# A vision-transformer block on one core: the remainder matmuls over the last 64 features, as pairs of 64-row tiles

## The chip, the cores and the metric

The kernel runs on one core of one Trainium2 chip. The metric is the device time of one execution in microseconds. The core has five engines with queues of their own: TensorE multiplies matrices (a weight load, then a matmul that streams columns against the loaded weights), VectorE and ScalarE work element by element, GpSimd does small work and indirect DMAs, SyncE issues DMAs. They are ordered among each other by semaphores that the kernel sets and waits for by hand.

## What is computed

Sixteen images of 3 x 112 x 112 are cut into 49 patches of 16 x 16 each; every patch becomes a token of 192 features. Then follow a self-attention with 12 heads of 64 and a feed-forward layer with 8 experts, of which each token goes to two. Cut to what matters:

```python
h = tok(x)                                   # [16, 49, 192], patches @ conv_w + position
y = layernorm(h)
q, k, v = y @ W_Q + b_Q, y @ W_K + b_K, y @ W_V + b_V
h = h + softmax(causal(q @ k.T / 8)) @ v @ W_O + b_O
x = layernorm(h)
top_p, top_i = top_k(softmax(x @ gate_w.T), 2)
for e in range(8):                           # up to 245 rows of one expert
    z = rms_norm(2 * rows[e]) * norm_w[e]
    g, u = split(z @ w13[e].T)               # 2 x 512 columns
    rows[e] = rows[e] + (silu(g) * u) @ w2[e].T
out = h + weighted sum of each token's two rows
```

## The kernel before

Tokens are worked on in 8 pairs of images, 98 tokens each (`PT`); the pairs 0 to 3 and 4 to 7 are the two halves. The 192 features are split in 128 (`DA`) and 64 (`DR`).

**Split products.** The products with W_Q, W_K, W_V and w13 take rounded 32-bit operands (f32r) in two pieces: a rounded value, and the rest that rounding left. The product of 128 features is made of three matmuls: value x value, value x rest, rest x value. For the last 64 features the pieces are stacked over the 128 partitions. `yR` (and `zeR` for the experts) holds the rounded values in the partitions 0 to 63 and the rests in 64 to 127; the weight tile `[.., 0, 1, ..]` holds the rounded weights twice, one copy above the other, and `[.., 1, 1, ..]` the rests of the weights, twice as well. One matmul with the first gives value x value and value x rest of the weights' values at once; a second one, with the second tile, adds rest x value, and rest x rest, which would not be needed.

So each output tile takes five matmuls. In `values(p)` (lines 340 to 344) they are for two banks of 384 columns each. In `queries_keys(half)` (L366 to L370) they are for 12 groups per half, 6 of queries and 6 of keys, of 400 columns each; the groups go round four banks of PSUM (0, 1, 4, 5), and a group waits for the evacuation of the group four before it. In `gate_up(e)` (L525 to L531) they are for 4 tiles `jt` of 128 hidden features, each with a gate and an up part (`u` 0 and 1) of 246 columns (`EC`) in one bank.

**Who makes the pieces.** ScalarE copies and rounds: `y_hi(p)` (L593, L594) after the transposes of y, and `x_hi(e)` (L717, L718) after those of the expert's rows. VectorE subtracts: `y_lo(p)` (L875, L876) and `x_lo(e)` (L1041, L1042). GpSimd clears `yA` and `yR` at the start (L760, L761).

**Who takes the results.** ScalarE evacuates the queries (L603) and values (L634) and applies silu to the gates (L724), VectorE evacuates the keys (L884) and multiplies gate and up (L1047). Each waits for a semaphore that the last matmul of the group raises: `qk_done`, `v_done`, `gu_done`.

**The order on TensorE.** Convolution of the pairs 0 to 3, transposes of y, some matmuls on a filler tile (L457), `queries_keys(0)`, and then a loop of steps s. A step has the transposes of the softmax for pair s (L393), the scores of pair s + 2 (L381 for the mask, over the whole array, and L386, 64 x 64 tiles, two heads side by side), the values of pair s + 1, the output projection of pair s - 1 (L416), the weighting with the values for pair s (L406, 64 x 64 tiles, two heads and two images at once), and small work for the choice of experts. Behind `values` stand L406 for five pairs, and for the pairs 0, 2 and 3 the matmuls L449, L416 and L327. `queries_keys(1)` runs in step 2, between. After all steps the rows come back from the scatter, and the experts run: `gate_up(0)`, then for each e `gate_up(e + 1)`, `transpose_x(e + 2)` (L511, L512) and `down(e)` (L544, 16 matmuls). The matmuls over plain 32-bit data (L386, L393, L406, L416, L544) show as two instructions for each call, except the transposes.

**The order on ScalarE in the expert stage.** For each e: `silu(e + 1, jt)` for four jt, with `split_hi(e + 2, jt)` (L669) behind the first two, then `x_hi(e + 2)` and `weigh(e)` (L736). VectorE has `gated`, `split_lo` and `x_lo` likewise. `gate_up(e)` waits for `x_hi` before its first matmul and for `x_lo` before its third (L529).

Of the kernel before, what the change touches and what calls it, by code (L numbers as in the profile page):

```python
# [22 lines left out]
TOK = PER_SIDE * PER_SIDE  # L23
D = 192
DA, DR = 128, 64
# [8 lines left out]
PT = 2 * TOK  # L34
# [20 lines left out]
def vit_block(nc, patches, conv_w, w_qkv, w_o, w13, w2, by_column, by_row, before, masking, blank, zeros, numbers, out):  # L55
# [6 lines left out]
    with ExitStack() as ctx:  # L62
# [30 lines left out]
        y = sb("y", [PT, 2, D])  # L93
        yA = sb("yA", [128, 2, PH, 128], f32r)
        yR = sb("yR", [128, PH, 128], f32r)
        qT = sb("qT", [128, HP, PH, 2, SLOT])
        kT = sb("kT", [128, HP, PH, 2, TOK])
        v = sb("v", [128, PH, QKV])
# [47 lines left out]
        toke = sb("toke", [EROWS, EXPERTS, 2], u32)  # L146
        zeA = sb("zeA", [128, 2, 2, EC], f32r)
        zeR = sb("zeR", [128, 2, EC], f32r)
        tokens_row = sb("tokens_row", [EROWS, N])
        member = sb("member", [EROWS, len(ONCHIP), N], f32r)  # L150
        yo = sb("yo", [EROWS, len(ONCHIP), 2, D], f32r)
# [150 lines left out]
        def _(pe):  # L302
# [27 lines left out]
            def values(p):  # L330

                pe.wait_ge(wlo_ready, 3)
                pe.wait_ge(ylo_ready, p + 1)
                if p >= 1:
                    pe.wait_ge(pt_ready, p)
                q = p % PH
                for j in range(2):
                    c = slice(384 * j, 384 * (j + 1))
                    o = ps[:, 2 + j, 0:384]
                    mm(o, yA[:, 0, q, :], wqkv[:, 2, 0, 0, c], start=True, stop=False)  # L340
                    mm(o, yA[:, 0, q, :], wqkv[:, 2, 1, 0, c], start=False, stop=False)
                    mm(o, yA[:, 1, q, :], wqkv[:, 2, 0, 0, c], start=False, stop=False)
                    mm(o, yR[:, q, :], wqkv[:, 2, 0, 1, c], start=False, stop=False)
                    last = mm(o, yR[:, q, :], wqkv[:, 2, 1, 1, c], start=False, stop=True)
                last.then_inc(v_done, 1)

            def queries_keys(half):

                pe.wait_ge(ylo_ready, PH * (half + 1))
                for n in range(2 * HP):  # L350
                    w, hp = n // HP, n % HP
                    if half and n == 2:
                        pe.wait_ge(z_ready, PH - 1)
                    if not half and hp == 0:
                        pe.wait_ge(wlo_ready, w + 1)
                    if n >= 4:
                        if n - 4 < HP:
                            pe.wait_ge(q_ready, HP * half + n - 3)
                        else:
                            pe.wait_ge(k_ready, HP * half + n - 3 - HP)  # L360
                    c = slice(128 * hp, 128 * (hp + 1))
                    o = ps[:, (0, 1, 4, 5)[n % 4], 0:2 * PH * EVEN].rearrange("p (s t) -> p s t", t=EVEN)

                    def tokens(t):
                        return t.rearrange("p a (i s) -> p (a i) s", i=2)[:, :, 0:EVEN]
                    mm(o, wqkv[:, w, 0, 0, c], tokens(yA[:, 0]), start=True, stop=False)  # L366
                    mm(o, wqkv[:, w, 0, 0, c], tokens(yA[:, 1]), start=False, stop=False)
                    mm(o, wqkv[:, w, 1, 0, c], tokens(yA[:, 0]), start=False, stop=False)  # L368
                    mm(o, wqkv[:, w, 0, 1, c], tokens(yR[:]), start=False, stop=False)  # L369
                    mm(o, wqkv[:, w, 1, 1, c], tokens(yR[:]), start=False, stop=True).then_inc(qk_done, 1)  # L370

            def scores(p):
                if p >= 1:
# [141 lines left out]
            def gate_up(e):  # L515
# [3 lines left out]
                for jt in range(JT):  # L519
                    if e >= 1:  # L520
                        pe.wait_ge(hT_ready, JT * (e - 1) + jt + 1)
                    for u in range(2):
                        o = ps[:, 2 + jt, u * EC:(u + 1) * EC]
                        w = slice(u * HID + 128 * jt, u * HID + 128 * (jt + 1))
                        mm(o, wsp[:, j, 0, 0, w], zeA[:, j, 0, :], start=True, stop=False)  # L525
                        mm(o, wsp[:, j, 1, 0, w], zeA[:, j, 0, :], start=False, stop=False)  # L526
                        if jt == 0 and u == 0:
                            pe.wait_ge(zelo_ready, e + 1)
                        mm(o, wsp[:, j, 0, 0, w], zeA[:, j, 1, :], start=False, stop=False)  # L529
                        mm(o, wsp[:, j, 0, 1, w], zeR[:, j, :], start=False, stop=False)  # L530
                        last = mm(o, wsp[:, j, 1, 1, w], zeR[:, j, :], start=False, stop=True)  # L531
                    last.then_inc(gu_done, 1)

            def down(e):
                j = e % 2
# [47 lines left out]
        def _(act):  # L583
# [6 lines left out]
            def y_hi(p):  # L590
                act.wait_ge(yt_done, p + 1)
                q, bank = p % PH, yt_bank(p)
                A(yA[:, 0, q, :].rearrange("q (i s) -> q i s", i=2)[:, :, 0:TOK], ps[:, bank, 0:PT].rearrange("q (i t) -> q i t", i=2), ACT.Copy)  # L593
                A(yR[0:DR, q, :].rearrange("q (i s) -> q i s", i=2)[:, :, 0:TOK], ps[0:DR, bank, 128:128 + PT].rearrange("q (i t) -> q i t", i=2),  # L594
                  ACT.Copy).then_inc(yhi_ready, 1)

            def queries_keys(half, some):
                for n in some:
# [115 lines left out]
            def x_hi(e):  # L714
                j = e % 2
                act.wait_ge(et_done, e + 1)
                A(zeA[:, j, 0, :], ps[:, j, 0:EC], ACT.Copy, scale=raw13[j][:, 2 * W13:2 * W13 + 1])  # L717
                A(zeR[0:DR, j, :], ps[0:DR, j, EC:2 * EC], ACT.Copy, scale=raw13[j][0:DR, 2 * W13 + 1:2 * W13 + 2]).then_inc(zehi_ready, 1)  # L718

            def silu(e, jt):  # L720
                act.wait_ge(gu_done, JT * e + jt + 1)
# [34 lines left out]
        def _(pool):  # L756
            P = nc.gpsimd
            P.memset(filler[:], 0.0).then_inc(filler_ready, 1)  # L758
            P.memset(mhalf[:], -0.5)
            P.memset(yA[:].bitcast(f32), 0.0)  # L760
            P.memset(yR[:].bitcast(f32), 0.0).then_inc(y_zeroed, 1)  # L761
            P.memset(qT[:], 0.0)
            P.memset(prob[:], 0.0)
# [394 lines left out]
```

## Time and profile before

| | |
|---|---|
| median of 3 runs | 217.92 us (217.6 to 218.06) |
| the profiled execution, its own time | 216.08 us |
| its span, from the first instruction to the last | 214.3 us |
| TensorE matmuls, busy | 193.9 us (91%), 1926 instructions |
| TensorE weight loads, busy | 175.6 us (82%) |
| VectorE busy | 125.3 us (58%) |
| ScalarE busy | 90.6 us (42%) |
| GpSimd busy | 66.8 us (31%) |
| TensorE's share of the chain that ended last | 75% |

In the rows below PE is the matmul part of TensorE, PEld its weight loads, DVE is VectorE, ACT ScalarE, POOL GpSimd; a q behind one is its queue. L with a number is the line of the kernel. Matmuls are pipelined and their ends are modelled: two that follow each other overlap in the rows, and busy time is not the same as time at full rate. The page of this profile gives the shares of the whole span; for the three edited places the views by stretch, and the starts of single instructions in them, say more.

### The profile page before, as it was taken

The page shows a single profiled execution, that of the slowest core. Times are in us where ns is not written, and L with a number is a line of the kernel's source. Part 1 is how long each engine was busy: PE and PEld are TensorE (multiplying, and loading weights), DVE is VectorE, ACT ScalarE, POOL GpSimd, SP SyncE. Part 2 cuts the span into 40 slices and gives each one's busy share as a digit, 9 for nine tenths or more (in the row PEclk, how much of TensorE's full clock was granted, in tenths as well). Part 3 has the DMA queues.
Part 4 walks back from the last instruction along what each step waited for, and adds up shares of the span by engine and source line. Part 5 has one row for each costly group of instructions (what it writes and reads, how often), then busy time and mean ns, then how long its engine had stood idle before and what let it go on. Part 6 is the DMA issues. An engine that isn't in the chain of part 4 may idle for free.

```text
span 214.3 us, 4932 instructions
## 1 busy us (share of the span) xinstructions
PE 193.9 (91%) x1926; PEld 175.6 (82%) x1926; DVE 125.3 (58%) x381; ACT 90.6 (42%) x186; POOL 66.8 (31%) x114
## 2 busy tenths in 40 slices
PE   6878999999989998999999859299999999999970
PEld 1865998998988996989999734289999999999960
DVE  0369365766465055997775872454584486495174
ACT  2064601215335511365487553156476567653110
POOL 9531000120135000266366877000225315514000
PEclk9999999999999999999999999979999999999996
DMA  6999990000014000001101001257187678513633
GB/s 191 401 401 432 309 360 24 2 3 0 3 25 163 35 3 0 14 20 33 32 0 32 26 23 27 85 188 279 18 313 244 204 254 266 161 32 110 161 67 114
DMA packets 11204, 27.07 MB, mean 126 GB/s; under 512 B 2661, under 2 KB 6498, under 8 KB 9998
## 3 DMA queue, kind: packets, MB, share of 16 engines
q1 hardware_dynamic: 8366, 24.10, 32.6%
q0 software_dynamic: 2304, 2.21, 3.7%
q10 hardware_dynamic: 512, 0.46, 0.8%
q8 instruction: 15, 0.25, 0.5%
q14 instruction: 7, 0.06, 0.1%
HBM read 23.95 MB, written 5.77 MB: 139 GB/s over the span
## 4 chain that ended last, share of the span: by engine, by line
PE 75%; DVE 7%; POOL 7%; DMA 4%; issue 4%; ACT 1%; DVEq 0%; SPq 0%; POOLq 0%; ACTq 0%
PE ps L544 10%; PE ps L386 6%; PE ps L416 6%; PE ps L314 5%; POOL slots L811 4%; PE ps L529 4%; PE ps L530 3%; PE ps L531 3%; PE ps L526 3%; PE ps L525 3%; PE ps L406 3%; PE ps L366 2%; DMA xp<-patches 2%; PE ps L368 2%; PE ps L369 2%
## 5 line engine op out<-in xcount | busy, mean ns | idle before, releaser
L836 POOL DMA_INDIRECT parts<-qT,toke x12 | 17.2, 1430 | 44.2 <-ACT qT L736 42.4
L811 POOL DMA_INDIRECT slots<-row,slot x16 | 18.0, 1122 | 29.2 <-issue 22.9
L974 DVE TENSOR_TENSOR wqkv<-raw,wqkv 128x1024 fp32r<-128x1024 f32 x16 | 19.5, 1222 | 7.6 <-DMA slots<-row,slot 4.4
L1047 DVE TENSOR_TENSOR v<-v,ps 128x246 f32<-128x246 f32 x32 | 12.5, 407 | 19.2 <-ACT v L724 19.2
L544 PE MATMUL ps<-xp,v 128*123 128x192 f32 x128 | 22.0, 326 | 0.0
L544 PEld LDWEIGHTS ps<-xp,v 128*123 128x123 f32 x128 | 20.6, 186 | 0.0
L525 PE MATMUL ps<-zeA,wqkv 128*128 128x246 f32 x64 | 19.0, 297 | 0.0
L630 ACT ACTIVATE prob<-sm 128x588 f32<-128x588 f32 x8 | 5.6, 706 | 31.0 <-DVE sm L895 31.0
L314 PE MATMUL ps<-convw,xp 128*98 128x192 f32 x96 | 16.9, 330 | 1.8 <-DMA xp<-patches 1.0
L724 ACT ACTIVATE v<-ps 128x246 f32<-128x246 f32 x32 | 12.0, 375 | 14.9 <-PE ps L531 13.4
L457 PE MATMUL ps<-filler 128*128 128x512 bf16 x62 | 17.1, 427 | 1.3 <-POOL filler L758 1.3
L529 PE MATMUL ps<-zeA,wqkv 128*128 128x246 f32 x64 | 18.0, 282 | 0.0
L531 PE MATMUL ps<-zeR,wqkv 128*128 128x246 f32 x64 | 17.9, 280 | 0.0
L530 PE MATMUL ps<-zeR,wqkv 128*128 128x246 f32 x64 | 17.9, 280 | 0.0
L526 PE MATMUL ps<-zeA,wqkv 128*128 128x246 f32 x64 | 17.8, 279 | 0.0
L314 PEld LDWEIGHTS ps<-convw,xp 128*98 128x98 f32 x96 | 15.1, 165 | 3.0 <-DMA xp<-patches 1.9
L416 PE MATMUL ps<-wo,zs 128*98 128x192 f32 x96 | 17.2, 329 | 0.0
L669 ACT ACTIVATE wqkv<-raw 128x1024 fp32r<-128x1024 f32 x16 | 16.9, 1053 | 0.0
L416 PEld LDWEIGHTS ps<-wo,zs 128*98 128x98 f32 x96 | 15.1, 165 | 0.7 <-issue 0.4
L884 DVE TENSOR_SCALAR kT<-ps,columns 128x392 f32<-128x392 f32 x12 | 7.5, 626 | 13.8 <-PE ps L370 13.8
L774 POOL TENSOR_SCALAR ve<-mv 98x1 f32<-98x1 f32 x8 | 2.2, 269 | 41.8 <-DVE mv L861 41.8
L386 PEld LDWEIGHTS ps<-kT,qT 64*64 64x64 f32 x384 | 12.4, 134 | 2.7 <-issue 1.2
(143 smaller groups left out, 483.8 us busy)
## 6 DMA issues: line engine op xcount, KB each, us to landing
raw<-w SPq DMA_DIRECT2D x8, 1025.0 KB, 6.3
xp<-w SPq DMA_DIRECT2D x8, 384.0 KB
xp<-patches SPq DMA_DIRECT2D x8, 294.0 KB, 5.8
raw<-w_qkv SPq DMA_DIRECT2D x3, 768.0 KB, 9.0
slots<-blank SPq DMA_DIRECT2D x8, 196.0 KB, 4.5
xp<-slots SPq DMA_DIRECT2D x8, 196.0 KB
parts<-zeros SPq DMA_DIRECT2D x1, 1176.0 KB, 8.7
part<-parts SPq DMA_DIRECT2D x4, 294.0 KB
```

Of the source, the lines that this page charges most:

```text
L314: last = mm(ps[0:PT, conv_bank(p), 0:D], xp[:, p % PH, c, :], convw[:, c, :], start=(c == 0), stop=(c == KC - 1))
L386: last = mm(ps[r, hp // 3, c:c + TOK], qT[r, hp, p % PH, i, :], kT[r, hp, p % PH, i, :], start=False, stop=(hp % 3 == 2 and i == 1))
L416: last = mm(ps[0:PT, 6, 0:D], zs[:, p % 2, c, :], wo[:, c, :], start=(c == 0), stop=(c == HP - 1))
L525: mm(o, wsp[:, j, 0, 0, w], zeA[:, j, 0, :], start=True, stop=False)
L526: mm(o, wsp[:, j, 1, 0, w], zeA[:, j, 0, :], start=False, stop=False)
L529: mm(o, wsp[:, j, 0, 0, w], zeA[:, j, 1, :], start=False, stop=False)
L530: mm(o, wsp[:, j, 0, 1, w], zeR[:, j, :], start=False, stop=False)
L531: last = mm(o, wsp[:, j, 1, 1, w], zeR[:, j, :], start=False, stop=True)
L544: last = mm(ps[0:EROWS, 6 + r, 0:D], hT[:, j, jt, r * EROWS:(r + 1) * EROWS], w2s[:, j, jt, :], start=(jt == 0), stop=(jt == JT - 1))
L811: P.indirect_dma_start(slots, bass.IndirectOffsetOnAxis(slot[:, p % PH, k:k + 1], 0), row[:, p % 2, k, :], None, bounds_check=EXPERTS * ST ...
L836: P.indirect_dma_start(parts, bass.IndirectOffsetOnAxis(toke[:, e, r:r + 1], 0), ye[0:EROWS, e % 2, r, :], None, bounds_check=TOPK * N + E ...
L974: last = V.tensor_tensor(wsp[:, j, 1, half, :], raw13[j][:, half * W13:(half + 1) * W13], wsp[:, j, 0, half, :].bitcast(f32), ALU.subtract)
```

## The change

Of the five matmuls of a group the last, with the rests of the weights, gives up its rest x rest half: only the 64 rows with the rounded values are left. Two groups' last matmuls are made a pair, one on the partitions 0 to 63 and one on 64 to 127, each with an output bank of its own. For the second the rounded values have to lie in the partitions 64 to 127, which is what the new tiles `yH` and `zeH` are for: ScalarE writes the same rounded values a second time. Pairs are: in `values` the two banks; in `queries_keys` groups n and n + 1; in `gate_up` the tiles jt and jt + 1, once for the gate and once for the up part. The semaphores of both groups of a pair are raised behind the pair, so the first group of a pair is released later than before. In `gate_up` only the first group in a bank starts with the flag that clears it, since both groups of a bank are open at the same time. GpSimd clears `yH` too.

```diff
@@ -93,6 +93,7 @@
         yR = sb("yR", [128, PH, 128], f32r)
+        yH = sb("yH", [128, PH, 128], f32r)
@@ -146,6 +147,7 @@
         zeR = sb("zeR", [128, 2, EC], f32r)
+        zeH = sb("zeH", [128, 2, EC], f32r)
@@ -341,8 +343,8 @@
                     mm(o, yR[:, q, :], wqkv[:, 2, 0, 1, c], start=False, stop=False)
-                    last = mm(o, yR[:, q, :], wqkv[:, 2, 1, 1, c], start=False, stop=True)
-                last.then_inc(v_done, 1)
+                mm(ps[:, 2, 0:384], yR[0:DR, q, :], wqkv[0:DR, 2, 1, 1, 0:384], start=False, stop=True)
+                mm(ps[:, 3, 0:384], yH[DR:128, q, :], wqkv[DR:128, 2, 1, 1, 384:768], start=False, stop=True).then_inc(v_done, 1)
@@ -367,7 +369,10 @@
                     mm(o, wqkv[:, w, 0, 1, c], tokens(yR[:]), start=False, stop=False)
-                    mm(o, wqkv[:, w, 1, 1, c], tokens(yR[:]), start=False, stop=True).then_inc(qk_done, 1)
+                    if n % 2:
+                        mm(pair, wqkv[0:DR, w, 1, 1, 128 * (hp - 1):128 * hp], tokens(yR[0:DR]), start=False, stop=True).then_inc(qk_done, 1)
+                        mm(o, wqkv[DR:128, w, 1, 1, c], tokens(yH[DR:128]), start=False, stop=True).then_inc(qk_done, 1)
+                    pair = o
@@ -522,14 +527,20 @@
-                        mm(o, wsp[:, j, 0, 0, w], zeA[:, j, 0, :], start=True, stop=False)
+                        mm(o, wsp[:, j, 0, 0, w], zeA[:, j, 0, :], start=(u == 0), stop=False)
...
-                        last = mm(o, wsp[:, j, 1, 1, w], zeR[:, j, :], start=False, stop=True)
-                    last.then_inc(gu_done, 1)
+                    if jt % 2:
+                        for u in range(2):
+                            w = [slice(u * HID + 128 * t, u * HID + 128 * (t + 1)) for t in (jt - 1, jt)]
+                            o = [ps[:, 2 + t, u * EC:(u + 1) * EC] for t in (jt - 1, jt)]
+                            first_of = mm(o[0], wsp[0:DR, j, 1, 1, w[0]], zeR[0:DR, j, :], start=False, stop=(u == 1))
+                            second = mm(o[1], wsp[DR:128, j, 1, 1, w[1]], zeH[DR:128, j, :], start=False, stop=(u == 1))
+                        first_of.then_inc(gu_done, 1)
+                        second.then_inc(gu_done, 1)
@@ -591,8 +602,9 @@
-                A(yR[0:DR, q, :].rearrange("q (i s) -> q i s", i=2)[:, :, 0:TOK], ps[0:DR, bank, 128:128 + PT].rearrange("q (i t) -> q i t", i=2),
-                  ACT.Copy).then_inc(yhi_ready, 1)
+                for rows_of in (yR[0:DR], yH[DR:128]):
+                    last = A(rows_of[:, q, :].rearrange("q (i s) -> q i s", i=2)[:, :, 0:TOK], ps[0:DR, bank, 128:128 + PT].rearrange("q (i t) -> q i t", i=2), ACT.Copy)
+                last.then_inc(yhi_ready, 1)
@@ -715,7 +727,9 @@
-                A(zeR[0:DR, j, :], ps[0:DR, j, EC:2 * EC], ACT.Copy, scale=raw13[j][0:DR, 2 * W13 + 1:2 * W13 + 2]).then_inc(zehi_ready, 1)
+                for rows_of in (zeR[0:DR], zeH[DR:128]):
+                    last = A(rows_of[:, j, :], ps[0:DR, j, EC:2 * EC], ACT.Copy, scale=raw13[j][0:DR, 2 * W13 + 1:2 * W13 + 2])
+                last.then_inc(zehi_ready, 1)
@@ -758,6 +772,7 @@
             P.memset(yA[:].bitcast(f32), 0.0)
+            P.memset(yH[:].bitcast(f32), 0.0)
             P.memset(yR[:].bitcast(f32), 0.0).then_inc(y_zeroed, 1)
```

## Rows read from the trace of the kernel before

**Rows 1.** The page, part 4: shares of the chain that ended last.

```profile
PE 75%; DVE 7%; POOL 7%; DMA 4%; issue 4%; ACT 1%; DVEq 0%; SPq 0%; POOLq 0%; ACTq 0%
```

**Rows 2.** Busy time by stretch, and TensorE's granted clock (PEclk, 1.00 is full).

```profile
core 0: us, PE busy (x) PEld busy (x) DVE busy (x) ACT busy (x) POOL busy (x), PEclk, DMA share, GB/s
20.20:31.90 11.70, 11.70 (x62) 11.27 (x60) 6.46 (x10) 4.68 (x8) 0.00 (x0) 1.00 0.97 347
...
141.00:204.00 63.00, 63.00 (x503) 63.00 (x502) 35.90 (x77) 33.81 (x72) 17.16 (x12) 0.99 0.59 191
```

**Rows 3.** The chain in order of time, attention: start, length in us, what.

```profile
99.60 0.85 PE ps L406 x48
...
102.70 0.83 PE ps L386 x24
```

**Rows 4.** Timeline, matmuls of `gate_up`: start, duration, engine, line, operation, shapes.

```profile
155.79 0.28 PE L531 MATMUL ps<-zeR,wqkv 128*128 128x246 f32 x1
...
156.37 0.28 PE L531 MATMUL ps<-zeR,wqkv 128*128 128x246 f32 x1
```

**Rows 5.** Timeline, matmuls of `queries_keys(0)`, one group.

```profile
22.02 0.35 PE L366 MATMUL ps<-yA,wqkv 128*128 128x400 f32 x1
...
22.98 0.36 PE L366 MATMUL ps<-yA,wqkv 128*128 128x400 f32 x1
```

**Rows 6.** Timeline, the end of `values` and the first 64 x 64 tiles behind.

```profile
90.62 0.34 PE L343 MATMUL ps<-wqkv,yR 128*128 128x384 f32 x1
90.80 0.34 PE L344 MATMUL ps<-wqkv,yR 128*128 128x384 f32 x1
91.06 0.45 PE L406 MATMUL ps<-probT,v 64*64 64x49 f32 x16
```

**Rows 7.** Groups by line and shape: count, busy us, mean ns of one, idle before.

```profile
L531 PE MATMUL ps<-zeR,wqkv 128*128 128x246 f32 x64 | 17.9, 280 | 0.0
...
L386 PE MATMUL ps<-kT,qT 64*64 64x49 f32 x384 | 14.4, 221 | 0.0
...
L344 PE MATMUL ps<-wqkv,yR 128*128 128x384 f32 x16 | 5.4, 337 | 0.0
```

**Rows 8.** Timeline, from the last 64 x 64 tiles to full matmuls.

```profile
37.80 0.22 PE L386 MATMUL ps<-kT,qT 64*64 64x49 f32 x2
37.95 0.44 PE L340 MATMUL ps<-wqkv,yA 128*128 128x384 f32 x1
38.23 0.33 PE L341 MATMUL ps<-wqkv,yA 128*128 128x384 f32 x1
```

**Rows 9.** A transpose behind 64 x 64 tiles (timeline), and the mean (groups).

```profile
82.96 0.33 PE L393 MATMUL ps<-columns,prob 128*128 128x128 f32 x1
...
L393 PE MATMUL ps<-columns,prob 128*128 128x128 f32 x48 | 6.7, 276 | 0.0
```

**Rows 10.** Timeline, `y_hi(7)` and the start of `queries_keys(1)`.

```profile
68.40 0.25 ACT L593 ACTIVATE yA<-ps 128x98 fp32r<-128x98 f32 x1
...
68.54 0.24 ACT L594 ACTIVATE yR<-ps 64x98 fp32r<-64x98 f32 x1
...
69.39 0.46 PE L366 MATMUL ps<-yA,wqkv 128*128 128x400 f32 x1 [0.36 <-DVE yR L876]
```

**Rows 11.** Timeline, `y_lo(3)` and the start of `queries_keys(0)`.

```profile
19.66 0.26 DVE L876 TENSOR_TENSOR yR<-ps,yR 64x98 fp32r<-64x98 f32 x1
...
20.01 0.43 PE L366 MATMUL ps<-yA,wqkv 128*128 128x400 f32 x1
```

**Rows 12.** Timeline, `x_hi` and `x_lo` of one expert, and their reader.

```profile
159.19 0.45 ACT L718 ACTIVATE zeR<-ps,raw 64x246 fp32r<-64x246 f32 x1
...
160.18 0.47 DVE L1042 SCALAR_TENSOR_TENSOR zeR<-ps,raw,zeR 64x246 fp32r<-64x246 f32 x1
...
161.46 0.28 PE L529 MATMUL ps<-zeA,wqkv 128*128 128x246 f32 x1
```

**Rows 13.** Timeline, GpSimd at the start.

```profile
2.12 0.53 POOL L761 MEMSET yR<- 128x512 f32 x1
...
9.36 0.19 POOL L774 TENSOR_SCALAR ve<-mv 98x1 f32<-98x1 f32 x1 [1.81 <-DVE mv L861]
```

## The prediction

> **What bounds the kernel now.** I read the chain of work that ended last first. TensorE carries three quarters of it, in small shares by line [rows 1]. So the second view is the busy time by stretch: in the first stretch of query and key matmuls (the second is alike) and in the whole expert stage TensorE is busy all of the time, at a granted clock of 1.00 and 0.99, while VectorE and ScalarE are busy for little over half of it at most [rows 2]. Between these the attention steps run nearly back to back on TensorE too: the chain there is TensorE's lines one after the other [rows 3]. The reader is to see that nearly every nanosecond that TensorE's queue gains or loses in the three edited places ends in the time, and that what other engines get on top is mostly under cover.
>
> **How the durations are read.** A matmul's duration is longer than what it occupies, since the next one starts while it drains. So the cadence counts, the distance of two starts: 0.58 us from L531 to the next L531 five matmuls on, 0.115 each [rows 4]; 0.96 for five of the 400-column matmuls of queries and keys, 0.192 each [rows 5]; 0.175 for the 384-column ones of `values` [rows 6]. The durations are 0.280 and 0.337 [rows 7] and 0.355 [rows 5], and they count wherever something has to wait for the end.
>
> **What the change removes.** 64 matmuls L531 become 64 of 64 rows, which run as 32 rounds of two; 24 of L370 become 12 rounds; 16 of L344 become 8 rounds. That two row halves do run side by side is seen in the trace: 48 matmuls L406, on four quarters of the array with outputs in two banks, take 0.85 us, 24 of L386 on two quarters take 0.83 [rows 3]. A pair of L386 so takes about twice the time per instruction of L406: what is set is the time of a round, not of an instruction. I take a round to have the cadence of the full matmul it replaces, since its 128 weight columns and its streamed columns are the same. The Trainium skill, page "TensorE: Matmul & The Clock Gate", section "LDWEIGHTS (loading the stationary operand)", says the same of the weights: the load goes by columns and not by rows; no row here separates the two.
>
> **What it adds: a change of the array's division, in and out.** The trace has some fifty places where a full matmul is followed by one on a quarter of the array or the other way round, and each has a gap. The last L344 at 90.80, first L406 at 91.06 [rows 6]: 0.27 where the cadence is 0.175. Last L386 at 37.80, first full matmul L340 at 37.95 [rows 8]: 0.15, where rounds of the same kind are some 0.06 apart (0.83 for twelve, of which 0.15 is the way out [rows 3]). Both gaps are the duration of the matmul before less 0.07 (0.337 - 0.07, 0.221 - 0.07 [rows 7]): the next one starts only when the array is nearly empty. And then its weights were not loaded ahead: L340 after the gap lasts 0.44, not 0.337, and the one behind it starts 0.28 later, not 0.175 [rows 8]. So each such change costs (duration - 0.07 - cadence) plus 0.10 of open weight load. Behind it L393, a transpose, shows only 0.33 for 0.276, so 0.05 [rows 9].
> The skill's page "TensorEngine Tiling (Array Packing)", section "Key Properties", puts it as a rule, and against this change: changing the tiling mode drains the TensorE. The trace agrees, with the 0.27 and 0.15 above. No row shows a tile of 64 rows by 128 columns, only 64 by 64; I take the same price, as the nearest row. Both ends for it: nothing, if halves by rows alone need no change (the first rival), and 0.10 for the weights in full.
>
> **Experts, L525 to L531.** Two blocks per expert, 16 in all. From the last full matmul to the first tile 0.21 + 0.10, second round 0.115, its second tile 0.01 later, then to the next full one 0.21 + 0.10: 0.745 us. Before, the same stretch held five cadences (one of its own and four L531): 0.575. So +0.17, x16 = 2.7. Behind six of the blocks stand the transposes of `transpose_x`, which show 0.05 and not 0.10: -0.3. Sum +2.4.
>
> **Queries and keys, L366 to L370.** 12 blocks of one round: 0.285 + 0.10, + 0.01, + 0.285 + 0.10 = 0.78, against three cadences, 0.58. +0.20, x12 = 2.4; the last block of each half is followed by the bf16 mask L381, whose weights are short (no open load taken): -0.2. Sum +2.2.
>
> **Values, L340 to L344.** 8 blocks. Three (p = 0, 2, 3) are followed by full matmuls: 0.37 + 0.01 + 0.37 = 0.75 against 0.525, +0.22 each, less about 0.1 in all for shorter weights behind: +0.6. Five are followed by L406, which pays its gap already now: 0.37 + 0.01 + 0.27 = 0.65 against 0.62, +0.03 each, +0.1 (if going from one kind of tile to another needs no gap, -0.1 each instead). Sum +0.7.
>
> **The second copy.** On ScalarE each `y_hi` and each `x_hi` gets one more activation. (a) `y_hi(7)`: its L593 and L594 (68.40, 68.54) stand in the chain to L366, which waited 0.36 us for `y_lo` [rows 10]; the three activations would start 0.14 apart as these two do, so +0.15. (b) `y_hi(3)`: its `y_lo` ended at 19.91, and L366 started at 20.01 behind the fillers [rows 11], so at most 0.1 of cover stands against 0.15 asked, and the weight load comes later too: +0.1. (c) `x_hi`, in every expert: L718 at 159.19; `x_lo` ends at 160.65 (L1042), and L529, which waits for it, starts at 161.46: 0.8 us of cover [rows 12]. (d) GpSimd's memset of `yH` is like that of `yR`, 0.53 us; GpSimd then waited 1.81 us for its first moments [rows 13], so nothing; without that cover 0.5. Together +0.3 for (a) and (b).
> The moved semaphores add no wait, but eat cover: `silu` of tiles 0 and 2 now wait for the next tile too. Queued behind the silu of tile 2 on ScalarE are that of tile 3 and `x_hi`; both silus start when the last tile is done. That puts `x_hi` back by about 0.2 and its third activation adds 0.36, while TensorE comes 0.1 later; of the 0.8 some 0.3 is left. If it were gone, six experts would pay what is missing. The next user of a bank in `gate_up` of the next expert comes over 2.6 us later (`down`, 16 of L544, lies between). In `queries_keys` banks are four deep: group n+4 starts a whole pair (1.9 us) after the release of n and n+1, whose two evacuations take some 1.2.
>
> **Sum.** 2.4 + 2.2 + 0.7 + 0.3 = +5.6 us. The profiled execution took 216.1 (span 214.3, 1.8 around it) and becomes 221.7; the median of the runs is 217.92 and becomes 223.5.
>
> **Rivals.**
> 1. No drain between whole rows and row halves (the tile is as wide as the array, and only the 64 by 64 ones pay). Then each round replaces two matmuls for good: 32 x 0.115 + 12 x 0.192 + 8 x 0.175 = 3.7 + 2.3 + 1.4 = 7.4 less, 0.3 for the copy: 217.9 - 7.1 = 210.8. For it: only 64 by 64 tiles are in the trace. Against: every change there, in and out, with bf16, f32 and rounded f32 neighbours, has the gap. It decides as soon as a block costs less than the two or four cadences that it frees, which is at about 0.17 us (experts) and 0.20 us less than the price taken. The time by the skill's table "Theoretical Speedup" of the tiling page (up to 2x for 64 rows) would be this one. Chance 0.12.
> 2. The drain, but weights loaded under it. Of 36 ways in and some 22 ways out with wide weights, 0.10 each, up to 5.8 us go: between 217.7 and 221, say 220. Against: the load of L340 is open after its gap [rows 8]. Chance 0.10.
> 3. The two halves don't run side by side, since each now takes all columns of the array. Then every round pays its cadence twice: +7.4 on the forecast, 230.9. For: L406 and L386 share the columns by halves. Against: in L406 upper and lower rows feed the same columns, in two banks, and still four run at once [rows 3]. Chance 0.05.
> Forecast with its mechanism: 0.73; its own range 221.5 to 225.5 (a fifth of each gap either way, and the cover of (c)).
>
> **Chances and range.** Less than 0.2% of 218 us, 0.4 us, a measurement of this kernel can't tell from no change. Faster: the first rival and a little of the second's lower end, 0.13. Same: 0.03, from that lower end. Slower: 0.84. The range reaches down over most of the second rival and up a little past the forecast's own: 219.0 to 226.5; left out are the first and third rival and the second's lowest end.
>
> **What would show it.** In the changed profile: starts of the row tiles, pairs 0.01 apart (else rival 3); 0.31 from L530 to where the first tile really streams and 0.21 from the last tile to the next full matmul (else rival 1); the matmul behind it at 0.38 instead of 0.28 (else rival 2). The way from one `down` to the next becomes 0.3 longer. TensorE's granted clock stays at 1.00 in these stretches; if it fell to half, all of this would be wrong. A wait of L529 for `zelo_ready` would show (c) gone.

## The result and the profile after

| | before | after |
|---|---|---|
| median (lowest to highest) | 217.99 us (217.6 to 218.17, 4 runs) | 223.35 us (222.45 to 224.28, 4 runs) |
| profiled execution, its own time | 216.08 us | 224.08 us |
| its span | 214.3 us | 222.1 us |

The ratio is 1.0249, 95% interval 1.0193 to 1.0304: slower, by 5.4 us in the medians, and clear of no change; that it is 2% or more is likely and not sure. The two profiled executions lie 8.0 us apart, and of that 1.7 are a matter of the start, as the table of stages shows.

The page of after, parts 1 and 4, first lines. Against [rows 1] the chain is made of the same engines.

```profile
PE 201.6 (91%) x1923; PEld 170.8 (77%) x1926; DVE 124.9 (56%) x381; ACT 94.8 (43%) x202; POOL 67.1 (30%) x115
...
PE 76%; DVE 7%; POOL 6%; DMA 4%; issue 4%; ACT 1%; DVEq 0%; SPq 0%; POOLq 0%; ACTq 0%
```

Busy time of after by stretch: first queries and keys, second, expert stage, as in [rows 2].

```profile
21.90:34.50 12.60, 12.55 (x61) 9.77 (x60) 5.88 (x8) 4.72 (x8) 0.00 (x0) 1.00 0.89 316
73.10:85.60 12.50, 12.50 (x60) 9.74 (x60) 2.32 (x4) 3.70 (x9) 0.35 (x1) 1.00 0.04 15
146.00:206.80 60.80, 60.80 (x458) 56.24 (x456) 36.36 (x77) 35.72 (x77) 17.03 (x12) 1.00 0.55 182
```

The matmul side is as full as before, and that is what misleads here: the weight loads, 11.27 of 11.70 us in [rows 2], are now 9.77 of 12.60. TensorE is not waiting for anybody there; it is between two ways of using its array. The granted clock is 1.00 in these three stretches.

One block of `gate_up` in after, by the timeline (start, duration, engine, line). It answers to [rows 4].

```profile
160.97 0.28 PE L534 MATMUL ps<-zeA,wqkv 128*128 128x246 f32 x1
161.09 0.27 PE L535 MATMUL ps<-zeR,wqkv 128*128 128x246 f32 x1
161.29 0.38 PE L540 MATMUL ps<-zeR,wqkv 64*128 64x246 f32 x1
161.29 0.38 PE L541 MATMUL ps<-zeH,wqkv 64*128 64x246 f32 x1
161.51 0.27 PE L540 MATMUL ps<-zeR,wqkv 64*128 64x246 f32 x1
161.51 0.28 PE L541 MATMUL ps<-zeH,wqkv 64*128 64x246 f32 x1
161.71 0.38 PE L530 MATMUL ps<-zeA,wqkv 128*128 128x246 f32 x1
161.94 0.27 PE L531 MATMUL ps<-zeA,wqkv 128*128 128x246 f32 x1
```

Read the starts: 0.20 from the last full matmul to the first tile, where the cadence is 0.115; the two tiles of a round start together; the second round 0.22 later, since the first tile's weights were loaded in the open (0.38 for 0.27); 0.20 to the next full one, again with its load in the open. From L535 to the second full matmul behind, 0.85 us; before, six cadences, 0.69.

One block of `queries_keys` and one of `values`, the same view; they answer to [rows 5] and [rows 6].

```profile
23.39 0.35 PE L371 MATMUL ps<-yR,wqkv 128*128 128x400 f32 x1
23.67 0.45 PE L373 MATMUL ps<-yR,wqkv 64*128 64x400 f32 x1
23.67 0.45 PE L374 MATMUL ps<-yH,wqkv 64*128 64x400 f32 x1
24.06 0.46 PE L368 MATMUL ps<-yA,wqkv 128*128 128x400 f32 x1
24.36 0.35 PE L369 MATMUL ps<-yA,wqkv 128*128 128x400 f32 x1
```

```profile
51.48 0.34 PE L345 MATMUL ps<-wqkv,yR 128*128 128x384 f32 x1
51.74 0.44 PE L346 MATMUL ps<-wqkv,yR 64*128 64x384 f32 x1
51.75 0.44 PE L347 MATMUL ps<-wqkv,yH 64*128 64x384 f32 x1
52.12 0.39 PE L411 MATMUL ps<-probT,v 64*64 64x49 f32 x12
```

The last row shows that from tiles of 64 x 128 to tiles of 64 x 64 the array empties as well: 0.37, of which 0.10 is the 64 x 128 tile's own open load.

The stages, from the starts of their first instructions in the two timelines, in us (the 5.9 ahead of the first convolution and the 6.7 between the first and the second row are alike in both and left out):

| stage | before | after | difference | forecast |
|---|---|---|---|---|
| first convolution to the first transposes of y | 5.93 | 7.62 | +1.69 | 0 |
| `y_hi(3)`: its transposes to the first queries | 1.47 | 1.73 | +0.25 | +0.1 |
| `queries_keys(0)` | 11.67 | 12.70 | +1.03 | +1.1 |
| steps up to `queries_keys(1)`, with four `values` and `y_hi(7)` | 37.71 | 38.44 | +0.73 | +0.8 |
| `queries_keys(1)` | 11.44 | 12.68 | +1.24 | +1.1 |
| steps up to the experts, with four `values` | 57.12 | 57.23 | +0.11 | +0.1 |
| first transposes of rows to the first `gate_up` | 2.56 | 2.98 | +0.42 | 0 |
| first `gate_up` to `combine` | 58.46 | 60.92 | +2.46 | +2.4 |
| the rest, from `combine` on | 15.31 | 15.23 | -0.08 | 0 |

Three rows hold differences that the edit did not make. The first is taken up below. In `queries_keys(1)` of before five matmuls take 0.945 us where they take 0.967 in `queries_keys(0)`, and four of the other profiles with the same five matmuls there have 11.70 us for the stage and not 11.44. Against those the changed kernel's 12.68 is +1.0, as in the first half. And at the head of the expert stage TensorE ran at its lower rate in both, but not over the same matmuls: in after for all eight transposes of rows (0.20 us apart), in before for the last of them (0.10 apart until then) and into the first `gate_up`.

### The profile page after: what moved, and what is told of

Same layout as the page of the kernel before. It is cut to its first block, busy times and chain, and to the rows that moved or that the text cites. A ratio compares the mean times of both kernels' runs of the same rounds, so it can differ in the third digit from the quotient of the medians.

```text
span 222.1 us, 4946 instructions
## 1 busy us (share of the span) xinstructions
PE 201.6 (91%) x1923; PEld 170.8 (77%) x1926; DVE 124.9 (56%) x381; ACT 94.8 (43%) x202; POOL 67.1 (30%) x115
## 4 chain that ended last, share of the span: by engine, by line
PE 76%; DVE 7%; POOL 6%; DMA 4%; issue 4%; ACT 1%; DVEq 0%; SPq 0%; POOLq 0%; ACTq 0%
PE ps L555 9%; PE ps L391 6%; PE ps L421 6%; PE ps L316 6%; PE ps L530 4%; PE ps L534 4%; POOL slots L826 4%; PE ps L531 3%; PE ps L535 3%; PE ps L368 3%; PE ps L540 3%; PE ps L411 2%; DMA xp<-patches 2%; PE ps L370 2%; PE ps L369 2%
## 5 line engine op out<-in xcount | busy, mean ns | idle before, releaser
L1062 DVE TENSOR_TENSOR v<-v,ps 128x246 f32<-128x246 f32 x32 | 12.2, 406 | 21.6 <-issue 11.1
L989 DVE TENSOR_TENSOR wqkv<-raw,wqkv 128x1024 fp32r<-128x1024 f32 x16 | 19.5, 1222 | 7.7 <-DMA slots<-row,slot 4.4
L316 PE MATMUL ps<-convw,xp 128*98 128x192 f32 x96 | 18.6, 352 | 1.8 <-DMA xp<-patches 1.0
L530 PE MATMUL ps<-zeA,wqkv 128*128 128x246 f32 x64 | 19.7, 307 | 0.0
L316 PEld LDWEIGHTS ps<-convw,xp 128*98 128x98 f32 x96 | 16.5, 179 | 3.3 <-DMA xp<-patches 1.9
L738 ACT ACTIVATE v<-ps 128x246 f32<-128x246 f32 x32 | 10.9, 373 | 18.1 <-PE ps L541 14.1
L534 PE MATMUL ps<-zeA,wqkv 128*128 128x246 f32 x64 | 18.5, 289 | 0.0
L531 PE MATMUL ps<-zeA,wqkv 128*128 128x246 f32 x64 | 17.7, 277 | 0.0
L535 PE MATMUL ps<-zeR,wqkv 128*128 128x246 f32 x64 | 17.7, 277 | 0.0
L462 PE MATMUL ps<-filler 128*128 128x512 bf16 x59 | 16.3, 425 | 1.5 <-POOL filler L772 1.3
L899 DVE TENSOR_SCALAR kT<-ps,columns 128x392 f32<-128x392 f32 x12 | 7.0, 621 | 17.5 <-PE ps L374 17.5
L391 PE MATMUL ps<-kT,qT 64*64 64x49 f32 x384 | 14.4, 221 | 0.0
```

The lines of the kernel that those rows point to most:

```text
L316: last = mm(ps[0:PT, conv_bank(p), 0:D], xp[:, p % PH, c, :], convw[:, c, :], start=(c == 0), stop=(c == KC - 1))
L391: last = mm(ps[r, hp // 3, c:c + TOK], qT[r, hp, p % PH, i, :], kT[r, hp, p % PH, i, :], start=False, stop=(hp % 3 == 2 and i == 1))
L530: mm(o, wsp[:, j, 0, 0, w], zeA[:, j, 0, :], start=(u == 0), stop=False)
L989: last = V.tensor_tensor(wsp[:, j, 1, half, :], raw13[j][:, half * W13:(half + 1) * W13], wsp[:, j, 0, half, :].bitcast(f32), ALU.subtract)
```

## The experiments

Theory: the loss is in the passages, TensorE emptying its array and loading weights in the open on the way into the tiles and out of them. Rivals: it is ScalarE's second copy with the later semaphores; or the row tiles don't gain side by side what was counted. Stages are compared inside the profiles; the medians have a spread of their own, which the last runs explain in part.

**The copies alone.** To the kernel before only this is added (and `yH` cleared):

```diff
+                for rows_of in (yR[0:DR], yH[DR:128]):
+                    last = A(rows_of[:, q, :]...)
...
+                for rows_of in (zeR[0:DR], zeH[DR:128]):
+                    last = A(rows_of[:, j, :]...)
```

> Only the second copy: yH and zeH are written by ScalarE (and yH cleared by GpSimd), and nobody reads them; all matmuls are those of the kernel before. Theory of the passages (the loss is TensorE changing the array's division, emptying it and loading weights in the open each time): +0.4 us against before in the profiled span, 0.26 at the start of the first queries and keys, 0.12 to 0.15 at the second, nothing in the expert stage. Rival (ScalarE's extra activations and the later semaphores carry the loss): most of the +6, of it 2 or more in the expert stage.

Measured: ratio 1.0032 (0.9993 to 1.0070). From the transposes of y (pair 3) to the first queries +0.26 us, as expected; the stretch up to the second queries and keys +0.26, twice what was expected; first `gate_up` to `combine` 58.46, as before. So in attention the copies carry 0.5 us.

That the expert stage shows nothing is chance. Here TensorE ran at full rate from the first transpose of rows on (granted clock 1.00 in the 4 us behind it), and in before it didn't (0.60 in 138 to 141 us). The fair comparison is a kernel of further below, with the five matmuls of before and full rate in this stretch. The third matmul of the first `gate_up`, which waits for `x_lo(0)`, comes 2.53 us after the first transpose there and 3.01 here, where a third activation stands ahead of `x_lo(0)`. The rows of the waits, first that kernel, then this one:

```profile
PE ps L529 <- DVE zeR L1042: 0.3, 1, 0.3
...
PE ps L531 <- DVE zeR L1048: 0.5, 1, 0.5
```

From the first transposes of rows to `combine` it is 60.03 us there and 60.48 here: +0.45, once. The copies carry up to 1 us, and still not the six.

**The expert stage alone.** Attention is as before; `zeH` and the pairs in `gate_up` are those of the change.

> The change in the expert stage alone (zeH, 16 blocks of two rounds); attention as before. Passages: from first gate_up to the end of the last one +0.16 us for each of 16 blocks, about 0.3 less in all for the transposes behind six of them: +2.3 to 2.6 us in the span. Rival (copies and semaphores): the same size here but as waits of TensorE inside the stage; there should be none.

Measured: ratio 1.0143 (1.0062 to 1.0224). First `gate_up` to `combine` +2.47, as in the whole change (+2.46), so the edits in attention and in the experts don't act on each other. The waits have no row for TensorE in this stage, as expected.

**Twice as many blocks, the same tiles.**

```diff
                     for u in range(2):
                         ... four full matmuls
+                        if jt % 2:
+                            ... the two tiles of this u
```

> Expert stage alone, the pair for the gates and the pair for the ups each as a block of its own behind its matmuls: 32 blocks of one round instead of 16 of two, the same matmuls. Passages: a block costs 0.31 to get in, 0.31 to get out and frees two cadences of 0.115, so +0.27 each against before, x32 = +8.7, less 0.3 for the transposes: +8.4 us against before, about +6 against the experts-only kernel with 16 blocks. Rival (copies and semaphores): as the 16-block kernel, +2.4. Rival (row tiles are slow by themselves): as the 16-block kernel, since the tiles are the same.

```profile
150.91 0.28 PE L531 MATMUL ps<-zeR,wqkv 128*128 128x246 f32 x1
151.12 0.38 PE L535 MATMUL ps<-zeR,wqkv 64*128 64x246 f32 x1
151.12 0.38 PE L536 MATMUL ps<-zeH,wqkv 64*128 64x246 f32 x1
151.43 0.38 PE L526 MATMUL ps<-zeA,wqkv 128*128 128x246 f32 x1
```

Measured: ratio 1.0365 (1.0285 to 1.0446); the stage +8.18 us. The timeline above has a block of one round: 0.21 in, 0.31 to the next full matmul. Same tiles, same copies, same work, only 32 blocks for 16: the loss goes with the number of passages, 5.7 us for 16 more, 0.36 each. (The kernel with 16 blocks has a second loss in its +2.47, told below; by single `gate_up` of the experts 2 to 6 it is 4.73 to 4.76 us before, 4.94 to 4.96 with two blocks and without that loss, 5.70 to 5.72 with four: 0.38 a block.)

**Both tiles on the same rows.**

```diff
-    second = mm(o[1], wsp[DR:128, j, 1, 1, w[1]], zeH[DR:128, j, :], ...)
+    second = mm(o[1], wsp[0:DR, j, 1, 1, w[1]], zeR[0:DR, j, :], ...)
```

> Expert stage alone, 16 blocks, but both tiles of a round take the upper 64 rows (zeR and the weights of the partitions 0 to 63; the result is the same, zeH is written and not read). So the two of a round can't run side by side. Passages, with rounds that overlap in the real change: two tiles a cadence of 0.115 apart instead of 0.003, two times a block: +0.23 a block, x16 = +3.6 us on top of the experts-only kernel, +6 against before. If the two halves do not run side by side anyway: no difference to the experts-only kernel.

```profile
147.56 0.28 PE L531 MATMUL ps<-zeR,wqkv 128*128 128x246 f32 x1
147.76 0.38 PE L536 MATMUL ps<-zeR,wqkv 64*128 64x246 f32 x1
147.98 0.28 PE L537 MATMUL ps<-zeR,wqkv 64*128 64x246 f32 x1
148.10 0.27 PE L536 MATMUL ps<-zeR,wqkv 64*128 64x246 f32 x1
148.22 0.27 PE L537 MATMUL ps<-zeR,wqkv 64*128 64x246 f32 x1
148.41 0.38 PE L526 MATMUL ps<-zeA,wqkv 128*128 128x246 f32 x1
```

Measured: ratio 1.0258 (1.0179 to 1.0337). The block is 0.85 long from L531 to L526, against 0.62 in the change: +0.23 a block, as expected. Now the tiles stand 0.115 apart, where those on different rows stood together, so running side by side is real and is worth what was counted. But the stage grew by 2.7 against the experts-only kernel and not by 3.6: `gate_up` of the experts 2 to 6 took 5.41 us each, for 5.10 to 5.13, +0.30 and not +0.46. Something in the experts-only kernel had already cost 0.17 there. In these five experts the third matmul is late. From the trace of after:

```profile
164.28 0.64 ACT L738 ACTIVATE v<-ps 128x246 f32<-128x246 f32 x2
164.63 1.22 DVE L989 TENSOR_TENSOR wqkv<-raw,wqkv 128x1024 fp32r<-128x1024 f32 x1
165.68 0.46 ACT L731 ACTIVATE zeH<-ps,raw 64x246 fp32r<-64x246 f32 x1
165.77 0.73 DVE L1062 TENSOR_TENSOR v<-v,ps 128x246 f32<-128x246 f32 x2
167.03 0.47 DVE L1057 SCALAR_TENSOR_TENSOR zeR<-ps,raw,zeR 64x246 fp32r<-64x246 f32 x1
167.37 0.27 PE L531 MATMUL ps<-zeA,wqkv 128*128 128x246 f32 x1
167.56 0.38 PE L534 MATMUL ps<-zeA,wqkv 128*128 128x246 f32 x1
```

`x_lo` (L1057) ends at 167.50, and L534 starts at 167.56 with its weights loaded in the open; from L531 to the matmul behind L534 it is 0.17 more than two cadences. No row of the waits lists it, since the modelled end of the matmul before covers the gap. What made `x_lo` late is on VectorE: the split of the next expert's weights (L989) runs until 165.85, then two products (L1062), and only then `x_lo`, which could have gone once `zeH` was written at 166.14. All of it is late from the start: counted from the start of the `gate_up` before, the silu of tile 0 begins at 2.77 us for 1.48 in before, since its semaphore now comes behind the pair, and `x_lo` ends at 8.46 for 7.17. That is 1.29 both times, while TensorE's own start of the next `gate_up` moved by 0.46.

**`x_lo` ahead of the last two products**, on the experts-only kernel:

```diff
-                for jt in range(JT):
-                    gated(e + 1, jt)
-                    if jt < 2:
-                        split_lo(e + 2, jt)
-                x_lo(e + 2)
+                for jt in range(2):
+                    gated(e + 1, jt)
+                    split_lo(e + 2, jt)
+                x_lo(e + 2)
+                for jt in range(2, JT):
+                    gated(e + 1, jt)
```

> The experts-only kernel (16 blocks) with one thing moved: VectorE does x_lo(e + 2) before the gate-times-up products of tiles 2 and 3 of expert e + 1, not behind them. In the changed kernel the third matmul of gate_up (L534) lasts 0.38 us and not 0.28 in the experts 2 to 6, just behind the end of x_lo. Theory of lost cover (the semaphores raised later push the weight split of the next expert and, behind it on VectorE, x_lo; TensorE waits 0.17 us in each of five experts): 0.85 us less from the first gate_up to the first combine than the experts-only kernel, 57.6 there becomes about 60.1 instead of 60.9. Theory that all of the loss lies in the passages: no difference.

```profile
171.50 0.41 PE L526 MATMUL ps<-zeA,wqkv 128*128 128x246 f32 x1
171.75 0.27 PE L527 MATMUL ps<-zeA,wqkv 128*128 128x246 f32 x1
171.86 0.28 PE L530 MATMUL ps<-zeA,wqkv 128*128 128x246 f32 x1
...
PE ps L551 <- DVE v L1056: 0.5, 1, 0.5
```

Measured: ratio 1.0125 (1.0062 to 1.0187), not to be told from the experts-only kernel's: as a whole the reordering gained nothing. The third matmul (here L530) is on time at 0.28, and the five `gate_up` took 4.94 to 4.96 us, 0.17 less each: the cause of the late third matmul is shown. The sum, though, missed: 61.2 us from first `gate_up` to `combine` and not 60.1. The two products pushed back in expert 6 are what `down(6)` waits for, and the stretch of `down(5)` and `down(6)` grew from 5.07 to 5.86 (the waits row shows 0.5 of it); the first two `gate_up` took 0.27 more. The gain was given back one step later.

**One block of four rounds.** Experts 1 to 6 (0 and 7 keep two blocks of two), with splits, one silu and `x_hi`/`x_lo` ahead of the other silus:

```diff
+                act.wait_ge(gu_done, JT * (e + 1))
+                for c in range(2):
+                    split_hi(e + 2, c)
+                silu(e + 1, 0)
+                x_hi(e + 2)
+                for jt in range(1, JT):
+                    silu(e + 1, jt)
...
                 (VectorE: split_lo twice, gated 0, x_lo, gated 1 to 3)
```

> Expert stage alone, with one block of four rounds in the experts 1 to 6 (two blocks of two in 0 and 7), the same tiles. For it ScalarE and VectorE do the splits of the next expert's weights, the silu of tile 0 and x_hi / x_lo before the silus of tiles 1 to 3. Passages: a block of four rounds costs 0.31 + 3 x 0.115 + 0.31 = 0.97 against nine cadences, 1.03: -0.06 each, six of them -0.4, less 0.3 for the transposes behind; the other four blocks +0.6. So 0 (-0.3 to +0.3) against before in the expert stage, 2.5 less than the experts-only kernel. Rival (row tiles or copies slow by themselves): as the experts-only kernel, +2.5.

Measured: ratio 1.0019 (0.9982 to 1.0055); first `gate_up` to `combine` 58.72 against 58.46, +0.26 and 2.2 below the experts-only kernel. Each `gate_up` of the experts 2 to 6 took 4.52 to 4.59 us, against 4.73 to 4.76 before. With a quarter of the passages of the kernel with 32 blocks, in these experts, the same tiles are a small gain. In it the waits have one row, `down(6)` waiting for VectorE's last product, 0.8 us. But the +0.26 flatters it: its first two `gate_up` took 9.59 us, for 10.07 in before at the lower rate. The fair test is the last kernel below.

**The start.** The first row of the table of stages has nothing to do with the edit: TensorE's work there is the same. The rows are 3.3 us of both traces, from the first convolution on, then the same stretch with more fillers (busy us and number of matmuls are the first pair behind the length; the third last column is the granted clock). In this order: before, after, before filled, after filled.

```profile
5.90:9.20 3.30, 3.29 (x20) 3.27 (x21) 1.01 (x4) 0.00 (x0) 1.65 (x5) 1.00 1.06 397
...
5.90:9.20 3.30, 3.28 (x10) 3.00 (x11) 0.16 (x1) 0.00 (x0) 2.11 (x5) 1.00 1.07 404
...
5.90:9.20 3.30, 3.30 (x21) 3.02 (x21) 0.90 (x3) 0.00 (x0) 1.64 (x5) 1.00 1.05 399
...
5.90:9.20 3.30, 3.30 (x19) 3.15 (x19) 0.80 (x3) 0.00 (x0) 2.10 (x5) 1.00 1.07 402
```

20 matmuls against 10 in the same time: in after they ran at half the rate, though the clock column says 1.00 for both (it is the cadence that tells: 0.32 us and 0.16). Before it, in both, TensorE had run eight fillers 0.43 us apart for 512 columns, which is the lower of its two rates (1.2 GHz), and then paused from 4.9 to 5.9 us. The experts-only kernel and that with both tiles on the same rows lost 1.0 and 1.9 us there, the copies-only kernel nothing. That it goes by execution and not by edit is seen in the times: the 23 of the unedited kernel beside the next run lie in two groups, nine from 215.4 to 216.1 us and fourteen from 217.2 to 218.1. The test fills the pause:

```diff
-            keep_busy(8, 0)
+            keep_busy(11, 0)
```

> The kernel before with 11 instead of 8 filler matmuls ahead of the first convolution. In all profiles so far the fillers end at 4.7 us and the first convolution starts at 5.7 to 5.9; then the convolution of the first pairs runs at the lower clock for 0 to 3.6 us more, by chance and whatever the kernel, and the 48 convolution matmuls take 5.9 to 7.9 us. Theory (the pause lets the clock's rise slip): 5.9 us every time, and a median about 1.2 us below that of before, 216.0 against 217.2, with a spread under 1 us. Rival (the chance has another cause): the same spread as before, no gain.

Measured: 215.95 us (214.78 to 216.57, 12 runs), before on the same chip 217.25 (215.37 to 218.05, 23 runs), ratio 0.9952 (0.9923 to 0.9981). The first row of the stages is 5.98 us. The median came as expected; the spread, 1.8 us, is less than the 2.7 of before and more than the 1 that was expected.

> The changed kernel with 11 instead of 8 filler matmuls ahead of the first convolution, the same edit as for the kernel before. Theory: the start takes 5.9 us every time; what is left against the filled kernel before is the change by itself, 0.26 + 0.12 for the copies, 2.2 for queries and keys, 0.7 for values, 2.9 in the expert stage, 6.2 us in all (forecast: 5.6). Rival (the start is part of what the change does): less than 5 us between the two filled kernels.

Measured: 222.20 us (222.05 to 222.48, 6 runs), ratio to before 1.0247 (1.0210 to 1.0284). Against the filled kernel before that is +6.25 us, 2.9%, with the start at 6.1 us; from the single times it is uncertain by some 0.4. So the change costs about 6.2 with the starts alike; between the medians of the unfilled kernels stood 5.4, with slow starts in either. That the number is the expected one is partly luck. `queries_keys` took +2.0 us and not +2.2, and the two profiles differ ahead of the experts: in the same 4 us from the first transpose of rows the granted clock was 0.64 in the filled kernel before and 1.00 in this one.

**A kernel faster than both.** First the other pause, ahead of the expert stage, on the filled kernel before:

```diff
-                    keep_busy((6, 6, 6, 18)[s - PAIRS + 1], 3)
+                    keep_busy((6, 6, 6, 28)[s - PAIRS + 1], 3)
```

> The kernel before with fillers in both pauses of TensorE: 11 instead of 8 ahead of the first convolution, and 28 instead of 18 in the last attention step, ahead of the wait for the experts' rows (2.3 us of pause in the profiles). Each of the 8 transposes behind the pause takes 0.10 instead of up to 0.20, and the first gate_up's run at the full clock from the start: from the first transpose to the first combine 59.6 us instead of 61.0 if the pause is what lets the clock fall, so about 214.7 against 217.2 of before. If the clock doesn't follow the pause: as with the first fillers alone, 216.0.

```profile
137.80:141.00 3.20, 3.04 (x13) 1.96 (x14) 1.79 (x8) 2.35 (x5) 0.00 (x0) 0.63 0.01 5
...
137.50:141.50 4.00, 3.65 (x27) 2.96 (x27) 2.26 (x8) 3.01 (x6) 0.00 (x0) 1.00 0.22 33
```

Measured: 215.01 us (214.59 to 215.59, 12 runs), ratio 0.9915 (0.9883 to 0.9947). The rows are that stretch in before, with a granted clock of 0.63, and in this kernel, with 1.00. From the first transpose to the first `combine` 60.0 us, for 61.0 (59.6 was expected).

> The same two fillers, and the changed kernel's tiles where they pay by the passages: in the experts 1 to 5 as one block of four rounds, with the order of splits, silus and x_hi / x_lo of the one-block kernel; all else with five full matmuls as before. Measured in the one-block kernel a gate_up of these experts took 4.52 to 4.59 us instead of 4.73, and the transposes behind 0.05 more: five times 0.07 to 0.15, so 0.3 to 0.8 us below the kernel with the two fillers, and no wait of TensorE ahead of down(6). If row tiles cost something by themselves that the one-block kernel hid: no gain.

Measured: 214.45 us (214.38 to 214.86, 6 runs), ratio to before 0.9885 (0.9837 to 0.9933), 8.9 us below the changed kernel's median, of which the fillers are a good part. The `gate_up` of the experts 2 to 5, with one block, took 4.52 to 4.59 us (that of expert 6, without one, 4.73), and `down(5)` with `down(6)` 5.07, no wait. The medians of this kernel and the one above are 0.56 us apart, as expected, and the stage 0.68 in the profiles; the runs of the two overlap, so the sign is likely and the size open.

## Why the prediction was right, and where it was not

**What bounds.** Held. In the edited stretches TensorE was full before and is full after, and each block's price went straight into the time. What did not hold is that the other engines' work stays under cover in the expert stage.

**The price of a passage.** Held, and on tiles that the trace of before didn't have. Into a block of `gate_up` 0.20 (forecast 0.21), `queries_keys` 0.28 (0.285), `values` 0.27 (0.27); the first tile's open load 0.10 (0.10); out 0.20 behind 246 columns, 0.39 behind 400 with the tile's own open load in it, and the matmul behind 0.10 longer (0.10). The rule taken from [rows 6] to [rows 8], the duration less 0.07, is the term that made the forecast. The rule of the Trainium skill, page "TensorEngine Tiling (Array Packing)", section "Key Properties", that a change of tiling mode drains the engine, so holds for 64 x 128 as well; the 0.28 and 0.20 above are this case's numbers for it.

**Rivals.** The first (no drain for halves by rows) falls with the 0.20 on either side of each block. The second (weights loaded under the drain) falls with the 0.38 of L540 and L530. The third (no side by side) falls twice: by the tiles' common start in after, and by the kernel with both on the same rows. The Trainium skill's page "TensorE: Matmul & The Clock Gate", section "Measured speedup vs the span model", gives tiles of a pack some 4 ns after one another; in after the second tile of a round starts within 0.01 us. The side-by-side run was never the trouble. A round saves one cadence, 0.115 us in `gate_up`, and a passage in and out costs over four.

**Queries and keys, values.** Forecast +2.2 and +0.7; measured +2.3, of which 0.2 is the quicker second half of before, and, with the steps around, +0.7. The five blocks before L406 cost 0.01 to 0.04 each, as told: that gap had been paid before.

**Experts.** The sum was right by errors against each other, which is luck. The passages were forecast at +2.4. By the kernel without the late `x_lo` two blocks cost an expert 0.21 in `gate_up` and 0.06 in the transposes behind, 0.27 for 0.29, and the stage 2.1. The step that failed is (c), the cover of `x_lo`, which was put at 0.8 us in every expert with 0.3 to be left. It failed twice.

In five experts 0.17 was missing, 0.85 in all. I had followed the silus of tiles 2 and 3 to ScalarE's `x_hi` and missed the other way: the silu of tile 0 comes 1.29 us later as well, behind it the split of the next expert's weights, and behind that VectorE's share of it and the last two products, all ahead of `x_lo` in VectorE's queue.

In expert 0 there is no such cover at all, since its third matmul comes right behind `x_lo(0)` as soon as TensorE runs at full rate. The second activation of `x_hi(0)` then costs 0.45. From the filled changed kernel, where the granted clock of this stretch was 1.00:

```profile
144.32 0.38 PE L534 MATMUL ps<-zeA,wqkv 128*128 128x246 f32 x1 [0.49 <-DVE zeR L1057]
```

At full rate the edit so costs 3.4 us from the first transposes of rows to `combine`: 60.03 in the kernel with both pauses filled, 63.46 in the filled changed kernel, which is 2.1, 0.85 and 0.45. Between the profiles of before and after it is 61.02 to 63.90, +2.9, and from the first `gate_up` on +2.46, because in before TensorE went through the first `gate_up` at the lower rate (10.07 us for the first two, where two at 4.75 take 9.5). That hid what (c) had left out.

**The second copy.** The size of a third activation was wrong: I let it start 0.14 behind the second, as the second does behind the first, and it starts 0.25 behind, at the second's end. (a) By the copies alone +0.26 for 0.15 forecast; in the whole change +0.12, but only since TensorE comes 0.14 later there. (b) +0.26 for 0.1: there was next to no cover. (d) nothing, as forecast: in the copies-only kernel the first queries came 0.26 late, all of it behind the last transposes of y.

**The sum.** 223.5 forecast, 223.35 measured, is closer than the working deserves. With the starts alike the change costs 6.2 and not 5.6, and more, about 7, against a kernel whose TensorE has full rate ahead of the experts too (222.20 and 215.01 us). The lost cover is most of what was missing. The medians had 5.4 because of the starts, and the profiles +2.46 in the experts because of the lower rate.

## What to carry to other kernels

A 64-row pair saves one matmul's cadence, and each group of pairs pays for emptying the array twice and for two open weight loads, here 0.5 us or more: count the groups and not the tiles, and gather tiles in blocks (here a block of one round loses 0.27 us and one of two 0.16, while one of four gains about 0.1). The price can be read from any place in a trace where full and small matmuls already follow each other. When a semaphore is raised later, follow every queue behind its waiter, not the one that ends nearest to it, and reckon that moving the work up only hands the wait to the next reader.

## What the runs showed that I had not expected

The convolutions at the start ran at half rate in some executions of kernels with the same work there, in one profile for over 4 us, behind a pause of 1.0 us of a TensorE that had not yet come up to its full rate. Three more filler matmuls in the pause took the spread of the kernel from 2.7 to 1.8 us and 1.3 us off its median. In that stretch the granted clock column reads 1.00 in both cases, so the number of matmuls per time has to be looked at beside it. Ahead of the expert stage the column does show it (0.63), and ten fillers there gave another 0.9 us. That the pause is the cause at the start rests on the profiles: of the eight with 8 fillers the first row of the stages took 5.9 us in two, 6.2 and 6.9 in two and 7.6 to 8.0 in four; of the four with 11 fillers it took 5.9 to 6.1. What decides it in a single execution stays open.
